# Moving norms, the first convolution tap and the product with D to ScalarE, and placing the rank counts between the pieces of the keys' split

## The reference, cut to what matters

```python
h = take(embed_matrix, x)
# layer 0, mixer: on layernorm(h)
xz = x @ W_in; xc, z = split(xz)
xc = silu(conv1d_causal(xc, conv_w, 3 taps) + conv_b);  z = silu(z)
y = cumsum(xc, axis=1) * BC + xc * D
h = h + (y * z) @ W_out
# layer 0, second half: on layernorm(h), normed once more with g1, b1
scores = sigmoid(normed @ Wr + br)
idx = top_k(-scores, 154)              # tokens that get attention
q, kk, v = normed @ Wq + bq, ...       # 12 heads of 16
attn_out = softmax(q kk / 4) v @ Wo + bo
pooled = einsum('bl,bld->bd', scores / sum(scores), normed)
mix_out = (normed + scores * pooled) @ Wm + bm
h2 = normed + where(selected, attn_out, mix_out)
h = h + h2 + gelu(layernorm(h2) @ W1 + bf1) @ W2 + bf2
# layer 1: full attention of 1024 tokens with a 100 slot memory, a gate,
# then two linear layers with quantised activations and weights
```

## Time and profile before

| | |
|---|---|
| median of 3 executions | 2289.93 us (2288.05 to 2291.09) |
| profiled execution | 2290.06 us, its span 2288.3 us |
| mean granted TensorE clock | 0.851 of full speed |
| TensorE busy | 1812.2 us, 79% |
| VectorE busy | 1454.4 us, 64% |
| ScalarE busy | 982.0 us, 43% |
| GpSimd busy | 119.8 us, 5% |

### The profile page before, as it was taken

The page is one execution under the profiler, slowest core; times in us unless marked ns, Lnnn a source line. Parts: engine busy times, 40 slices in busy tenths (PEclk is TensorE's granted clock), DMA queues, the critical chain, the costliest instruction groups (busy, mean ns, idle before and its releaser), DMA issues.

```text
span 2288.3 us, 27535 instructions
## 1 busy us (share of the span) xinstructions
PE 1812.2 (79%) x9834; PEld 957.4 (42%) x9834; DVE 1454.4 (64%) x3296; ACT 982.0 (43%) x1371; POOL 119.8 (5%) x163
## 2 busy tenths in 40 slices
PE   1786778998999899984566787899889898998735
PEld 1365447662333233353244554756423322333613
DVE  4747774047777677747667767522577767774786
ACT  0331331234666466641532234121466655667143
POOL 4010000000000000004011000000000000000010
PEclk9977785997999799996577778789889998999856
DMA  5011110012000010000000111000300100000000
GB/s 127 0 45 31 43 29 0 1 51 67 22 22 22 18 25 22 8 1 25 4 28 1 56 43 46 2 1 0 111 15 23 25 23 15 22 21 1 1 0 28
DMA packets 57644, 58.48 MB, mean 26 GB/s; under 512 B 27063, under 2 KB 35556, under 8 KB 57510
## 3 DMA queue, kind: packets, MB, share of 16 engines
q1 hardware_dynamic: 55894, 53.57, 9.2%
q0 software_dynamic: 1616, 3.16, 0.6%
HBM read 38.51 MB, written 18.16 MB: 25 GB/s over the span
## 4 chain that ended last, share of the span: by engine, by line
PE 57%; DVE 35%; issue 3%; ACT 3%; SPq 1%; DMA 1%; POOL 0%; DVEq 0%; ACTq 0%
DVE nmp L1419 9%; PE PV L803 8%; PE S L760 7%; PE ST L784 6%; PE ST L530 4%; PE ST L718 4%; DVE nmp L1351 3%; PE S L755 2%; PE MT L810 2%; DVE Er L1447 2%; PE S L615 2%; PE PV L643 2%; DVE st L1254 2%; PE S L729 2%; DVE R L1467 1%
## 5 line engine op out<-in xcount | busy, mean ns | idle before, releaser
L1419 DVE TENSOR_REDUCE nmp<-S 128x1 f32<-128x512 f32 x768 | 493.3, 686 | 120.5 <-PE S L760 116.4
L1087 ACT ACTIVATE Er<-ST 128x1024 f32<-128x1024 f32 x384 | 391.5, 1024 | 254.3 <-PE ST L784 246.7
L760 PE MATMUL S<-KS,QS 96*128 96x512 bf16 x768 | 316.1, 417 | 66.0 <-DVE nmp L1419 40.9
L784 PE MATMUL ST<-QS,KS 100*128 100x512 bf16 x768 | 238.7, 393 | 5.1 <-ACT QS L1078 3.6
L760 PEld LDWEIGHTS S<-KS,QS 96*128 96x128 bf16 x768 | 75.1, 98 | 327.2 <-DVE nmp L1419 243.0
L803 PE MATMUL PV<-Er,V 128*17 128x512 f32 x1536 | 205.4, 607 | 0.0
L1351 DVE TENSOR_REDUCE nmp<-S 80x1 f32<-80x512 f32 x192 | 120.7, 679 | 29.1 <-PE S L615 26.2
L615 PE MATMUL S<-KS,QS 96*80 96x512 bf16 x192 | 88.5, 498 | 32.3 <-DVE nmp L1351 22.2
L430 POOL TENSOR_SCALAR tp<-mv 128x8 f32<-128x8 f32 x20 | 5.1, 257 | 1998.7 <-DVE mv L1258 1998.7
L784 PEld LDWEIGHTS ST<-QS,KS 100*128 100x128 bf16 x768 | 68.8, 100 | 93.1 <-issue 48.7
L1407 DVE TENSOR_REDUCE junk<-S 128x68 f32<-128x272 f32 x96 | 42.4, 442 | 101.0 <-PE S L755 101.0
(11 more groups left out here) (363 smaller groups left out, 3173.5 us busy)
## 6 DMA issues: line engine op xcount, KB each, us to landing
KS<-scr_k SPq DMA_DIRECT2D x576, 32.0 KB, 1.8
scr_k<-R SPq DMA_DIRECT2D x16, 576.0 KB, 4.0
QS<-scr_q SPq DMA_DIRECT2D x288, 32.0 KB, 1.8
scr_q<-R SPq DMA_DIRECT2D x8, 576.0 KB, 4.9
out_dram<-HS SPq DMA_DIRECT2D x8, 384.0 KB, 2.8
QS<-scr_q SPq DMA_DIRECT2D x48, 30.0 KB, 1.9
wf<-in_L_ffn_W_dram SPq DMA_DIRECT2D x2, 576.0 KB
scr_q<-small SPq DMA_DIRECT2D x8, 90.0 KB, 2.0
```

The lines of the kernel that those rows point to most:

```text
L760: ins = nc.tensor.matmul(S[n % 2][:, :], QS[0:KP, h % KRING, (u // 2) * P:(u // 2 + 1) * P], KS[0:KP, h % KRING, (u % 2) * HALF:(u % 2 + 1 ...
L784: ins = nc.tensor.matmul(ST[i % 2][:, (kt % 2) * HALF:(kt % 2 + 1) * HALF], KS[0:KP + 4, h % KRING, kt * P:(kt + 1) * P], queries, start=T ...
L1087: A_(E[:, g, :], ST[i % 2][:, :], ACT.Exp).then_inc(s["exps"], 1)
L1419: v.tensor_reduce(nmp[:, u // 2, u % 2:u % 2 + 1], S[n % 2][:, :], AX.X, ALU.max).then_inc(s["reduced"], 1)
```

## The change

Five edits, all in layer 0 or the norms:

- `normalise` for norms 0 to 3 goes from VectorE to ScalarE, as eight Identity activations per sequence with a scale and a bias column. GpSimd makes the bias column `nb` (minus mean times scale) in two more operations. In ScalarE's order both sequences are normed before either is evacuated.
- The first tap goes to ScalarE (`first_tap`), behind the four outputs of `inproj` of its sequence. VectorE keeps the other two.
- The product with D goes to ScalarE, behind the Silu in `conv`, into `o.YD`, which lies in `o.X`.
- On TensorE `logits` loses the projection of the keys: both sequences' logits come first, then both `scores_row`, then both projections, which now wait for ScalarE's copy of the score row. ScalarE's exponentials and row copies come in that order too.
- On VectorE the counts go between the pieces: after the first subtraction of piece i, and the last one of piece i - 1, come the counts of tiles 2i and 2i + 1. `pool_tokens` comes ahead of the cut.

```diff
@@ -179,6 +179,7 @@
             o.Z = R[0:CH, 3076:3076 + L]
+            o.YD = o.X[0:CH, :, :].rearrange("p t d -> p (t d)")[:, 0:L]
             o.spl = R[0:CH, 0:3 * L].bitcast(BF16).rearrange("p (a c n) -> p a c n", a=3, c=2)
@@ -432,16 +434,16 @@
                 g.wait_ge(o.s["stats"], p * 5 + n + 1)
-                ins = rsqrt(o, o.rn[:], o.mv[:, :, 1], LN_EPS)
-                if second is None:
-                    ins.then_inc(o.s["rstd"], 1)
-                    return
-
-                link(ins)
-                link(g.tensor_tensor(o.tp[:], o.mv[:, :, 1], o.rn[:], ALU.mult))
-                link(g.tensor_tensor(o.rnn[:], o.tp[:], o.rn[:], ALU.mult))
-                link(rsqrt(o, o.rnn[:], o.rnn[:], second))
-                g.tensor_tensor(o.rnn[:], o.rnn[:], o.rn[:], ALU.mult).then_inc(o.s["rstd"], 1)
+                link(rsqrt(o, o.rn[:], o.mv[:, :, 1], LN_EPS))
+                scale = o.rn
+                if second is not None:
+                    scale = o.rnn
+                    link(g.tensor_tensor(o.tp[:], o.mv[:, :, 1], o.rn[:], ALU.mult))
+                    link(g.tensor_tensor(o.rnn[:], o.tp[:], o.rn[:], ALU.mult))
+                    link(rsqrt(o, o.rnn[:], o.rnn[:], second))
+                    link(g.tensor_tensor(o.rnn[:], o.rnn[:], o.rn[:], ALU.mult))
+                link(g.tensor_tensor(o.nb[:], o.mv[:, :, 0], scale[:], ALU.mult))
+                g.tensor_scalar(o.nb[:], o.nb[:], -1.0, None, ALU.mult).then_inc(o.s["rstd"], 1)
@@ -574,11 +576,9 @@
                 ins.then_inc(s["logit"], 1)
-                project(p, o, 0, wk, 0, o.XT, HALF, 2)
...
                 pe.wait_ge(s["score"], at(p, o, 1, 1))
-                pe.wait_ge(o.s["resid"], p * 14 + 4)
                 for t in range(T):
@@ -598,7 +598,6 @@
                 pe.wait_ge(s["nts"], at(p, o, 2, 2))
-                pe.wait_ge(s["srow_copied"], at(p, o, 1, 1))
                 project(p, o, 4, wq, 0, o.NTS, 2 * QP, 1)
@@ -916,6 +915,9 @@
                 for o in slots:
+                    pe.wait_ge(s["srow_copied"], at(p, o, 1, 1))
+                    project(p, o, 0, wk, 0, o.XT, HALF, 2)
+                for o in slots:
                     pick(p, o)
@@ -1029,9 +1031,22 @@
+            def first_tap(p, o, c):
+                act.wait_ge(o.s["inproj_out"], p * 8 + 4 * c + 4)
+                A_(o.Y1, o.XC[:, c, 2:L + 2], ACT.Identity, scale=convw[:, c, 2:3], bias=cols[:, c, 0:1]).then_inc(o.s["tap"], 1)
+
             def conv(p, o, c):
...
                 A_(o.Y1, o.Y1, ACT.Silu).then_inc(o.s["silu"], 1)
+                act.wait_ge(o.s["silu"], p * 4 + 2 * c + 1)
+                A_(o.YD, o.Y1, ACT.Copy, scale=cols[:, c, 1:2]).then_inc(o.s["silu"], 1)
+
+            def normalise(p, o, n, src, scale):
+                act.wait_ge(o.s["rstd"], p * 5 + n + 1)
+                for t in range(T):
+                    ins = A_(o.X[:, t, :], src[:, t, :], ACT.Identity, scale=scale[:, t:t + 1], bias=o.nb[:, t:t + 1])
+                    if t % 4 == 3:
+                        ins.then_inc(o.s["xnorm"], 1)
@@ -1115,21 +1130,27 @@
                 for o in slots:
+                    normalise(p, o, 0, o.U, o.rn)
+                for o in slots:
                     evac(p, o, 0, o.XT)
...
                         inproj(p, o, c)
+                        first_tap(p, o, c)
                     for o in slots:
                         conv(p, o, c)
+                for o in slots:
+                    normalise(p, o, 1, o.HS, o.rnn)
                 for o in slots:
...
                     A_(o.sc1[:], o.O[:, 0:T], ACT.Exp, scale=-1.0).then_inc(s["expz"], 1)
-                    cut(p, o, 0, pieces_k0(o), HALF)
                 for o in slots:
...
                     A_(o.srow, o.ST[:, :], ACT.Copy).then_inc(s["srow_copied"], 1)
+                for o in slots:
+                    cut(p, o, 0, pieces_k0(o), HALF)
                 for o in slots:
@@ -1146,10 +1167,14 @@
                 for o in slots:
+                    normalise(p, o, 2, o.U, o.rn)
+                for o in slots:
                     evac(p, o, 2, o.XT, 4, 5)
...
                         gelu(p, o, half)
+                for o in slots:
+                    normalise(p, o, 3, o.HS, o.rn)
                 for o in slots:
@@ -1258,14 +1283,7 @@
-            def normalise(p, o, n, src, scale):
-                ve.wait_ge(o.s["rstd"], p * 5 + n + 1)
-                for t in range(T):
-                    ins = v.tensor_scalar(o.X[:, t, :], src[:, t, :], o.mv[:, t, 0:1], scale[:, t:t + 1], ALU.subtract, ALU.mult)
-                    if t % 4 == 3:
-                        ins.then_inc(o.s["xnorm"], 1)
-
-            def cut(p, o, group, pieces, width):
+            def cut(p, o, group, pieces, width, between=None):
@@ -1283,32 +1301,36 @@
                         low(i - 1)
+                    if between is not None:
+                        between(i)
                 low(group + len(pieces) - 1)
...
                     link(v.memset(o.XC[:, :, 0:2], 0.0))
-                link(v.tensor_scalar(o.Y1, o.XC[:, c, 2:L + 2], convw[:, c, 2:3], cols[:, c, 0:1], ALU.mult, ALU.add))
+                ve.wait_ge(o.s["tap"], p * 2 + c + 1)
                 link(v.scalar_tensor_tensor(out=o.Y1, in0=o.XC[:, c, 1:L + 1], scalar=convw[:, c, 1:2], in1=o.Y1, op0=ALU.mult, op1=ALU.add))
...
             def gate(p, o, c):
-                ve.wait_ge(o.s["silu"], p * 2 + c + 1)
+                ve.wait_ge(o.s["silu"], p * 4 + 2 * c + 1)
                 link(v.tensor_tensor_scan(o.CUM[:, c, :], o.Y1, o.Y1, 0.0, ALU.add, ALU.bypass))
-                link(v.tensor_scalar(o.Y1, o.Y1, cols[:, c, 1:2], None, ALU.mult))
-                link(v.scalar_tensor_tensor(out=o.CUM[:, c, :], in0=o.CUM[:, c, :], scalar=cols[:, c, 6:7], in1=o.Y1, op0=ALU.mult, op1=ALU.add))
+                ve.wait_ge(o.s["silu"], p * 4 + 2 * c + 2)
+                link(v.scalar_tensor_tensor(out=o.CUM[:, c, :], in0=o.CUM[:, c, :], scalar=cols[:, c, 6:7], in1=o.YD, op0=ALU.mult, op1=ALU.add))
                 ve.wait_ge(o.s["inproj_out"], p * 8 + 4 * c + 4)
...
-            def rank_tokens(p, o):
+            def count_less(p, o, tiles):
                 ve.wait_ge(s["srow_copied"], at(p, o, 1, 1))
-                for t in range(T):
+                for t in tiles:
                     v.tensor_scalar(junkr[:, 0:L - t * P], o.srow[:, t * P:L], o.sc[:, t:t + 1], 0.0, ALU.is_lt, ALU.add, accum_out=o.cnt[:, 0, t:t + 1])
...
                                                 accum_out=o.cnt[:, 2, t:t + 1]))
+
+            def rank_tokens(p, o):
                 link(v.tensor_tensor(o.rank[:], o.cnt[:, 0, :], o.cnt[:, 1, :], ALU.add))
@@ -1493,8 +1515,6 @@
                     stats(p, o, o.U)
-                for o in slots:
-                    normalise(p, o, 0, o.U, o.rn)
                 for c in range(2):
@@ -1508,16 +1528,17 @@
                 for o in slots:
-                    normalise(p, o, 1, o.HS, o.rnn)
-                for o in slots:
                     ve.wait_ge(s["expz"], at(p, o, 1, 1))
...
                     v.reciprocal(o.sc[:], o.sc1[:]).then_inc(s["score"], 1)
-                    ve.wait_ge(s["score"], at(p, o, 1, 1))
-                    cut(p, o, 0, pieces_k0(o), HALF)
-                for o in slots:
+                for o in slots:
+
+                    def between(i, p=p, o=o):
+                        count_less(p, o, (2 * i, 2 * i + 1))
+
+                    pool_tokens(p, o)
+                    cut(p, o, 0, pieces_k0(o), HALF, between)
                     rank_tokens(p, o)
-                    pool_tokens(p, o)
                 for o in slots:
@@ -1528,7 +1549,6 @@
                 for o in slots:
-                    normalise(p, o, 2, o.U, o.rn)
                     link(v.tensor_tensor(o.HS[:], o.HS[:], o.U[:], ALU.add))
@@ -1536,8 +1556,6 @@
                             stats(p, o, o.HS)
-                for o in slots:
-                    normalise(p, o, 3, o.HS, o.rn)
                 for o in slots:
```

More of the change, by code:

```diff
@@ L159, in build @@
         wsum = sb("wsum", [P, 2])
-        OWN = """gathered stats rstd xnorm turned evac inproj inproj_out conv silu gated proj hi resid mid lo vproj vcopied
+        OWN = """gathered stats rstd xnorm turned evac inproj inproj_out tap conv silu gated proj hi resid mid lo vproj vcopied
             hidden gelu ffn h2 bhid bgelu hss hrms hquant hturned hcopied bout outs stored kw0 kw1 qw0 qw1""".split()
@@ L210, in build @@
             o.rnn = sb("rnn" + nx, [P, T])
+            o.nb = sb("nb" + nx, [P, T])
             o.tp = sb("tp" + nx, [P, T])
```

## The result

The changed kernel takes **2372.82 us** (median of 4 executions, 2370.56 to 2374.88) against 2290.51 us (2288.05 to 2291.70) for the kernel before on the same chip: a ratio of 1.0363, interval 1.0348 to 1.0377. It is 3.6% slower. Its profiled execution took 2374.88 us, span 2373.1 us, 84.8 us more than the span before. The mean granted TensorE clock fell from 0.851 to 0.834.

The account below looks back on a forecast made before the run. The chain that ended last was read as TensorE 57%, VectorE 35%, ScalarE 3%, then priced stage by stage. Pair 0's 34.0 and pair 1's 35.6 us gave 69.6 on 2290.1: 2360 us, range 2318 to 2382.

Parts of the forecast that it names:

- The large term: Logits to ranks, from first logits to second pick: +14.4 us in pair 0 and +16 in pair 1.
- the convolution: Input projection's start to last gate: +1.1 us a pair, bounds -2 and +4; VectorE's 6.2 us less work buys nothing.
- the norm before the FFN: Statistics to FFN start: +3.8 us a pair, bounds +2.5 and +5, for z's bias, ScalarE's norm and the evacuations.
- the selected attention: Attention stages between the edited places: stay as they are, only moved in time, no term in the sum.
- rival 3: TensorE's pauses before projections and in the convolution keep 1.2 GHz after restarts, tiles at 0.5 us: 2385 us; chance 0.07.
- ScalarE's order at the norms: All four norms: z's last norm tile directly before a's first evacuation; projections start 4 to 6 us later against z's statistics.
- Logits to ranks: Logits and score rows precede keys: first piece at 37.2 us, VectorE then bound for 43.9, second pick at 81.1.
- The distance of 22.8 us: First K piece must reach VectorE earlier than this after logits start (20.2 in pair 1) for its relief to pay.
- Rival 1: Logits and score rows at 2.4 GHz as the clock rises in the long run: about 2320 us; chance 0.17.
- then six outputs of 1.72 us follow up to 31.7: Convolution's second half: after TensorE's banks wait for a's copies, six projection outputs end 31.7 us after the projection's start.
- VectorE's residual addition [...] is no longer ahead, and is included since the start is absolute: Norm before the FFN: the addition that came between needs no separate term within the +3.8 us.
- The sum: Both pairs' terms: 34.0 us in pair 0 and 35.6 in pair 1, together +69.6 us.

## Why the prediction was right, point by point

The forecast was 2360 us, slower, and the time is 2372.82, inside its range. The large term held; the convolution, the norm before the FFN and the selected attention did not, and the errors do not cancel: the two largest that go the other way are worth 6 us. The time lies midway between the forecast and the 2385 us of rival 3, more clock loss, which had a chance of 0.07.

**ScalarE's order at the norms** was right: the last norm tile of z stands directly ahead of the first evacuation of a. +5.0, +5.9 and +3.8 before the input projection, the logits and the last projections came as +5.3 to +5.5, +5.1 to +5.4 and +4.0. The tile took 0.444 us and not my 0.40. The 0.7 us on 16 tiles are within the bounds. The estimate from the Trainium skill (ScalarE: Activation LUTs, What ACT_TABLE_LOAD costs) was 0.44, and the trace agrees with it. The reason given was too narrow in one place: before the input projection the number came true, but taking a through norm and evacuation first won at most 0.6 us there, so its 5 us do not hang on the order of a and z. What is left is that ScalarE now does norms and evacuations one behind the other, with slower tiles; how the 5 us divide between the two, no run shows.

**Logits to ranks** was right in its mechanism and a little high in size. Foreseen: first piece at 37.2 us after the first logits, second pick at 81.1. Measured: 35.0 and 77.8. The clock was up for part of a's logits (5.20 us, not 6.9), and VectorE needed 42.8 us for its chain, not 43.9. The distance of 22.8 us at which the edit would begin to pay was put to the test with 17.9, and it paid. Rival 1, a clock that rises in a long run without gap, is refuted: 0.50 over 18 us in which TensorE was busy for 18.00. As the forecast already said of the rule in the Trainium skill (TensorE: Matmul & The Clock Gate, What's actually happening), the trace speaks against it, now over a stretch almost three times as long.

**The convolution** is the first step that failed: +1.1 foreseen, +4.3 and +4.6 measured. Its order was right, down to the 4 us pause, but the step "then six outputs of 1.72 us follow up to 31.7" priced them at the clock before the pause. They ended 34.7 us after the start (93.60 + 13.37 - 72.30), and that is 3.0 of the 3.2 us. I had named the loss of clock and left it in the bound of +4, which the measured values pass. So the mechanism of rival 3 holds in this stage, at 3 us a pair; behind the pause the granted clock was 0.50 for 4 us. The 2.4 us behind the last gate in pair 0 are clock too, but can't be laid to the pause: the first four groups of eight matmuls of the output projection took 2.6 to 2.9 us each, 9.43 us after TensorE's last work, where before, after 11.40 us, only the first two took more than 1.6. In pair 1 the kernel before had four such slow groups as well, after 11.39 us, and there the difference is 0.4.

**The norm before the FFN** is the second: +3.8 foreseen, +6.6 measured, 2.9 us of it from GpSimd's tiny operations running beside VectorE's addition. The step that failed is "VectorE's residual addition [...] is no longer ahead, and is included since the start is absolute": that it would now run at the same time as the scale was the consequence to price.

**The selected attention** was said to be only moved in time. It took 103.19 us and not 98.22 in pair 0, with as many matmuls (653) and TensorE busy 86.60 us in place of 79.33, at a granted clock of 0.70 in place of 0.79. Over both pairs of all runs the same code gives between 97.8 and 103.3 us. In the run with the product with D alone it took 102.3 us in pair 0 and 98.2 in pair 1; the granted clock of the two was nearly alike up to 80 us into the stage, and in the next 8 us it was 0.50 and 1.00. What decides this was not isolated, and stays open; that it is worth up to 5 us a stage is measured.

**The sum** was 69.6, the spans differ by 84.8. Of the 15.2 missing, convolution and output projection are 9.5, the selected attention 7.1, the FFN's norm 5.6, while logits to ranks (-3.6) and the mix (-2.6) go the other way; what is left is under 1 us.

## What to carry to other kernels

Before moving work off a busy engine, look at whether the queue that it joins feeds the next stage: here ScalarE empties TensorE's banks, and each operation put ahead of an evacuation came out as a pause or a later start. Filling an engine's idle time needs its inputs to come no later for it: the same interleaving lost 12 to 15 us a pair with its keys at 35.0 us and won 4 to 7 with them at 17.9, so work out the break-even distance first. Price the matmuls behind a new pause at both clocks and keep the two as bounds, and expect a few us won upstream to be partly lost again in the next stage.

## What the runs showed of the hardware beyond that

- A GpSimd operation on a 128x8 tile slows down while VectorE adds two tensors from SBUF: 0.24 us became 1.65, 1.67 became 3.14; with the addition held back they are at 0.24 and 1.67. The Trainium skill states the cause (GPSIMD Engine Reference, Specifications: the SBUF interfaces are shared with VectorE, with contention when it has two SBUF inputs), and the trace agrees.
- TensorE was granted 0.50 for 18 us without a gap, in matmuls of one column and the transposes of the two score rows; 32 pooled matmuls took 5.17 us there and 2.80 behind a projection of 512 columns that had run at 1.00.
- The same 24 matmuls of the input projection took 12.2 to 13.6 us behind all ten pauses of 4.0 to 4.3 us in the runs (six outputs of 1.72 us, 10.3, without a pause). Behind pauses of 2.0 to 2.8 us they took 12.2 to 13.9 in pair 0 and 10.5 to 10.6 in pair 1, in each of three kernels.
